# A six-layer mixer on one core: linear-attention stages over three tiles and one instead of two and two, and a new order of all steps

## What is computed

```
x = x + _L0_xattn_ref(_layernorm(x), ctx_1024, ...)        # local cross attention, 512 keys per batch
x = x + _L0_attn_ref(_layernorm(x), ...)                   # a decaying scan over time
x = x + _L0_ffn_ref(_layernorm(x), ...)                    # shared network and 2 of 8 experts
x = x + _L1_xattn_ref(_layernorm(x), ctx_1024, ctx_1024, mask, ...)   # full attention, 16 heads, masked
x = x + _L1_attn_ref(_layernorm(x), ...)                   # linear attention and a 512-wide network
x = x + _L1_ffn_ref(_layernorm(x), ...)                    # 1 of 16 experts, 32 slots each
```

```
ln1 = layer_norm(x, gamma1, beta1)
q, k, v = ln1 @ wq, ln1 @ wk, ln1 @ wv                     # 16 heads of 8
qp, kp = relu(q) + 0.001, relu(k) + 0.001
kvs = einsum('blhm,blhd->bhmd', kp, v)                     # per batch and head
num = einsum('blhm,bhmd->blhd', qp, kvs)
den = einsum('blhm,bhm->blh', qp, sum(kp, axis=1))
add1 = (num / den) @ wo + x
h = gelu(layer_norm(add1) @ w1 + b1)
out = gelu(h @ w2 + b2) + add1
...
pos = cumsum(onehot, axis=0) - 1                           # a token's place in its expert: counts all tokens before it
keep = pos < cap
```

## Time and profile before

| | us |
|---|---|
| median of 3 runs | 247.67 (247.62 to 248.0) |
| the profiled execution | 247.71 |
| its span | 245.6 |
| PE busy | 224.0 (91%) |
| DVE busy | 179.5 (73%) |
| ACT busy | 133.0 (54%) |
| POOL busy | 28.9 (12%) |

### The profile page before, as it was taken

The page is one execution under the profiler, slowest core; times in us unless marked ns, Lnnn a source line. Parts: engine busy times, 40 slices in busy tenths (PEclk is TensorE's granted clock), DMA queues, the critical chain, the costliest instruction groups (busy, mean ns, idle before and its releaser), DMA issues.

```text
span 245.6 us, 5281 instructions
## 1 busy us (share of the span) xinstructions
PE 224.0 (91%) x1996; PEld 157.9 (64%) x1996; DVE 179.5 (73%) x518; ACT 133.0 (54%) x289; POOL 28.9 (12%) x47
## 2 busy tenths in 40 slices
PE   7899999998998997669799999989999888898995
PEld 6322785585965866436568666657667677787485
DVE  2574716999857389999786978998988757834672
ACT  2205651274566073579999796979858361133030
POOL 3010001010223033021302210010000111201000
PEclk9999999999999599999999999999999999999999
DMA  7999949200000000060004200000008998000001
GB/s 220 419 435 423 429 152 227 60 0 0 4 0 0 0 3 1 0 167 7 0 3 109 65 4 3 0 4 0 3 0 344 434 451 358 3 0 0 3 3 43
DMA packets 2904, 26.87 MB, mean 109 GB/s; under 512 B 448, under 2 KB 704, under 8 KB 1344
## 3 DMA queue, kind: packets, MB, share of 16 engines
q1 hardware_dynamic: 2880, 26.54, 29.8%
HBM read 26.28 MB, written 0.26 MB: 108 GB/s over the span
## 4 chain that ended last, share of the span: by engine, by line
PE 61%; DVE 21%; issue 9%; ACT 4%; POOL 1%; DMA 1%; POOLq 0%; DVEq 0%; ACTq 0%
PE bank L1403 9%; PE bank L1389 6%; PE bank L1279 5%; PE bank L1257 5%; PE bank L1218 4%; DVE ctx_sb L946 4%; PE bank L1419 4%; PE bank L1362 2%; PE bank L1202 2%; PE bank L1345 2%; PE bank L1614 2%; PE bank L1288 2%; PE bank L1604 1%; PE bank L1588 1%; ACT ctx_sb L557 1%
## 5 line engine op out<-in xcount | busy, mean ns | idle before, releaser
L557 ACT ACTIVATE ctx_sb<-ctx_sb,small_sb 128x512 f32<-128x512 f32 x64 | 46.0, 722 | 13.3 <-DVE small_sb L946 13.1
L946 DVE CUSTOM_DVE_ANT_0 ctx_sb<-bank,mask_sb 128x512 f32<-128x512 f32 x64 | 41.8, 683 | 4.0 <-PE bank L1389 3.9
L1403 PE MATMUL bank<-early_sb,ctx_sb 128*128 128x128 f32 x256 | 35.8, 278 | 3.1 <-ACT work_sb L568 1.8
L1403 PEld LDWEIGHTS bank<-early_sb,ctx_sb 128*128 128x128 f32 x256 | 27.8, 141 | 14.3 <-ACT ctx_sb L557 7.8
L377 POOL TENSOR_TENSOR rstd_sb<-veps_sb,minus_half_sb 128x2 f32<-128x2 f32 (+1 forms) x13 | 10.3, 791 | 145.9 <-DVE veps_sb L643 117.0
L568 ACT COPY work_sb<-bank 128x512 f32<-128x512 f32 x40 | 22.5, 577 | 3.9 <-PE bank L1403 3.7
L1389 PE MATMUL bank<-k_sb,work_sb 32*128 32x512 f32 x128 | 18.6, 639 | 3.9 <-DVE small_sb L946 3.9
L706 DVE SCALAR_TENSOR_TENSOR work_sb<-bank,early_sb,work_sb 128x512 f32<-128x512 f32 x16 | 11.9, 747 | 9.4 <-PE bank L1257 8.9
L1222 PEld LDWEIGHTS bank<-late_sb,ctx_sb 128*128 128x128 f32 x128 | 15.2, 191 | 5.1 <-issue 5.0
L957 DVE COPY work_sb<-bank 128x512 f32<-128x512 f32 x24 | 16.5, 687 | 2.7 <-PE bank L1403 2.7
L1222 PE MATMUL bank<-late_sb,ctx_sb 128*128 128x128 f32 x128 | 16.4, 280 | 1.6 <-DVE v_sb L749 1.4
(11 more groups left out here) (260 smaller groups left out, 396.5 us busy)
## 6 DMA issues: line engine op xcount, KB each, us to landing
k_sb<-moe_w SPq DMA_DIRECT2D x1, 4096.0 KB, 12.5
ctx_sb<-moe_w SPq DMA_DIRECT2D x1, 4096.0 KB, 15.7
ctx_sb<-ctx SPq DMA_DIRECT2D x3, 1024.0 KB, 15.2
late_sb<-late SPq DMA_DIRECT2D x1, 2966.5 KB, 21.7
mask_sb<-ctx_tok SPq DMA_DIRECT2D x1, 2048.0 KB, 13.2
v_sb<-ctx_tok SPq DMA_DIRECT2D x1, 2048.0 KB, 27.6
mask_sb<-mask SPq DMA_DIRECT2D x4, 512.0 KB, 8.3
mask_sb<-mask SPq DMA_DIRECT2D x8, 256.0 KB, 4.5
```

The costliest lines, as they stand in the source:

```text
L557: s.activation(sc[u % NSC], sc[u % NSC], ACT.Exp, bias=smin[:, u:u + 1], scale=-1.0, accum_out=rsum[:, u:u + 1]).then_inc(sig("p1_ready"), 1)
L946: v.tensor_tensor_reduce(sc[u % NSC], bank[SB[u % GROUPS]][:, :], mask[:, KEYS * b:KEYS * (b + 1)], MASK_BIG, 3e38, ALU.add, ALU.min, smin ...
L1403: last = nc.tensor.transpose(bank[TB[u % 2]][:, P * k:P * (k + 1)], sc[u % NSC][:, P * k:P * (k + 1)], wt("ident"))
```

## The change

Stream c takes tiles 0 to 2 (twelve batches), d tile 3 (four batches). Both have buffers of their own, and c can start only when 48 of the 64 exponentials are done. In c, the values are copied to SBUF by ACT and masked for four batches at once on POOL, three times; key-value products, their masks and denominators run for three tiles; the four hidden products go one by one through one bank, each with bias and GELU in one ACT operation from PSUM, where before two banks were filled by two products each and a GELU over all four followed. In both stages: the second of the two norms is formed directly by one power of var * (1 + eps) + eps * eps' (the first no longer has to be multiplied in), so that POOL does two powers of one column a tile and the three DVE steps between fall away; the bias b2 goes in by a product with the identity and the GELU reads PSUM; key sums are read in PSUM; the token dispatch mask is formed with the test for capacity in one operation. In d the gate's bias goes in by a product as well. Heads are taken for batches 12 to 14 and for 15 apart, the last from another bank. `dispatch(0, j)` moves to the end of c. Copies of transposed units go to DVE for 2 in 8 units, not 3. All four orders are new, from the first steps on.

The diff, cut (the orders of DVE, ACT and POOL, and slices that only follow the new tile counts, are left out):

```diff
 TURNS = {
     "PE": (
-        "L2 P L10 P L P5 L P L8 P L2 a L2 P L3 a L2 a3 L P L P7 L P L a L6 a L a2 L P a b P2 a3 b a3 b P b P "
-        "a P a P2 S P4 T S b P S T2 b T b T2 S V T b T b T2 S b T2 b V T b S T b3 T2 V T2 V S T b T2 b T S T2 "
-        "V T2 V S T4 V T2 c T2 S V T2 S T2 V T2 c T2 S V T4 c S V T2 c T2 c S V T2 c S T2 c T2 c T2 c S V c V "
-        "T2 c T2 V T2 c V c d3 c G8 d c d4 G d G3 d G2 d c d c G6 c G d G2 d6 G4 d G2 d2 G5 d G4 d19 "),
+        "L2 P L10 P L P5 L P L8 P L2 a L2 P L3 a L2 a2 L a L P7 L P2 L a L5 a L a2 L P2 a L P a P a2 b a3 b "
+        "P2 b a b a P2 S P2 S P2 T b P S T4 b T b T2 S V T b T S V b T2 b V b S T b T2 b3 T4 S V T2 b T S T2 "
+        "b T V T V T2 S T2 V T2 S T2 V T2 S T4 S V T2 V T2 S T2 V T2 c T2 V T2 S V c T2 S T2 c T c V c T2 S T "
+        "c T2 V c T2 c V c d2 c d G c G c d4 G d G c G c d3 c G c d c d c2 d3 G2 c G c d G3 d G4 c d2 G7 c2 "
+        "d19 "),
...
+        LT, LB = (range(0, 3), range(3, 4)), (12, 4)
+        def lcols(h):
...
-        mg = [kvs, mask[:, MH:MH + 4 * HTOK]]
-        ksum = small[:, 832:832 + HB]
+        def linear_buffers(n, at, rd):
+            (qp, att, qk, kp_tok, add1, res4, g2, vb, kvs), end = part(mask, [P * n] * 7 + [4 * P * n] * 2, at)
+            return (qp, att, qk, kp_tok, add1, res4, g2, vb, kvs, small[:, rd:rd + HEADS * n]), end
+        lin0, at = linear_buffers(3, 0, 560)
+        assert at <= MH + MH // 2
+        lin1, at = linear_buffers(1, MH + MH // 2, 608)
+        assert at <= CTX
+        lin = (lin0, lin1)
...
-        BY_DVE = (1, 4, 7)
+        BY_DVE = (3, 7)
...
             def linear_stages(h):
-                inverse_std(h, tiles_of(h), extra=True)
-                yield
...
+                yield
+                inverse_std(h, LT[h])
+                yield
+                for t in LT[h] if not h else ():
+                    pool.wait_ge(sig("vt_ready"), 1)
+                    g.tensor_tensor(vb[:, 512 * t:512 * (t + 1)].rearrange("p (b d) -> p b d", b=4),
+                                    att[:, P * t:P * (t + 1)].unsqueeze(1).broadcast_to([P, 4, P]),
+                                    wt("batchof").unsqueeze(2).broadcast_to([P, 4, P]), ALU.mult).then_inc(sig("vb_ready"), 1)
+                    yield
+                inverse_std(h, LT[h])
+                yield
+                g.tensor_tensor(res4, x_tok[:, lcols(h)], add1, ALU.add).then_inc(sig("res_ready"), 1)
+                yield
+                inverse_std(h, LT[h])
                 yield
...
             def linear_stages(h):
-                A, B = XL[h], YL[h]
-                normT(h, lnT[:, cols(h)], A[:, HTOK:], scale=wt("gamma"), bias=wt("beta"))
...
+                normT(h, lnT[:, c], turnedT, scale=wt("gamma"), bias=wt("beta"))
                 yield
                 act.wait_ge(sig("vtok_ps"), h + 1)
-                if h:
-                    s.copy(vb[:, 0:HTOK], B[:, 0:HTOK]).then_inc(sig("vtok_ready"), 1)
...
-                normT(h, lnT[:, cols(h)], A[:, HTOK:], scale=wt("gamma"), bias=wt("beta"))
+                s.copy(vb[:, 0:P] if h else att, B[:, 0:NT]).then_inc(sig("vtok_ready" if h else "vt_ready"), 1)
+                yield
+                normT(h, lnT[:, c], turnedT, scale=wt("gamma"), bias=wt("beta"))
                 yield
                 for n in range(4):
-                    act.wait_ge(sig("ffh_ps"), 2 * h + n // 2 + 1)
-                    s.activation(hT[:, HTOK * n:HTOK * (n + 1)], (B, A)[n // 2][:, HTOK * (n % 2):HTOK * (n % 2 + 1)],
-                                 ACT.Gelu if h else ACT.Identity, bias=wt("b1")[:, n:n + 1]).then_inc(sig("ffh_ready"), 1)
-                    yield
-                if not h:
-                    act.wait_ge(sig("ffh_ready"), 4)
-                    s.activation(hT, hT, ACT.Gelu).then_inc(sig("gelu_ready"), 1)
-                    yield
-                act.wait_ge(sig("ffo_ready"), h + 1)
-                s.activation(g2, g2, ACT.Gelu).then_inc(sig("g2_ready"), 1)
-                yield
-                normT(h, lnT[:, cols(h)], A[:, HTOK:])
+                    act.wait_ge(sig("ffh_ps"), 5 + n // 2 if h else n + 1)
...
                 ts = slice(tiles.start, tiles.stop)
+                if extra is not None:
+                    second = slice(TT + tiles.start, TT + tiles.stop)
+                    norms[h] += 1
+                    v.tensor_scalar(veps[:, second], ag3[:, ts, 1], 1.0 + extra, eps * extra, ALU.mult, ALU.add)\
+                        .then_inc(sig(f"ln_var{h}"), 1)
+                    yield
...
-                    v.tensor_scalar(veps[:, second], veps[:, second], extra, None, ALU.add).then_inc(sig(f"ln_var{h}"), 1)
+                v.tensor_scalar(veps[:, ts], ag3[:, ts, 1], eps, None, ALU.add).then_inc(sig(f"ln_var{h}"), 1)
...
+            def normalize_once(ch, h, src3, tiles, dst3):
+                dve.wait_ge(sig(f"ln_rstd{h}"), norms[h])
                 for t in tiles:
                     ch.add(v.tensor_scalar(dst3[:, t, :], src3[:, t, :], ag3[:, t, 0:1], rstd[:, t:t + 1],
                                            ALU.subtract, ALU.mult))
...
+                for n, (lo, hi) in enumerate(TAKE):
+                    dve.wait_ge(sig("o1_ready"), hi)
+                    src = bank[OB1][:, 0:P * (hi - lo)] if n < 4 else bank[OB2][:, 0:P]
+                    o = src.rearrange("p (b j q) -> p b j q", b=hi - lo, j=4)
+                    to = oT[:, SEQ * lo:SEQ * hi].rearrange("p (b q) -> p b q", b=hi - lo)
...
-                dve.wait_ge(sig("qk_ps"), h + 1)
...
-                ch.join()
-                dve.wait_ge(sig("vtok_ps"), h + 1)
+                dve.wait_ge(sig("oT_ready"), 5 if h else 3)
+                v.tensor_tensor(oT[:, c], oT[:, c], A[:, 0:NT], ALU.mult).then_inc(sig("o1T_ready"), 1)
+                yield
+                dve.wait_ge(sig(f"xo{k}_ps"), 4)
                 if not h:
-                    v.tensor_tensor(vb[:, 0:512].rearrange("p (b d) -> p b d", b=4),
-                                    vtok(0).unsqueeze(1).broadcast_to([P, 4, P]),
-                                    wt("batchof").unsqueeze(2).broadcast_to([P, 4, P]), ALU.mult).then_inc(sig("vb_ready"), 1)
-                    yield
+                    dve.wait_ge(sig("xb0_ready"), 2)
+                dve.wait_ge(sig("xb1_ready"), 2)
+                residual((ZL[1] if h else B)[:, 0:NT], xb_tok[:, c], k, c)
...
                 dve.wait_ge(sig("ksum_ps"), h + 1)
-                ch.add(v.tensor_copy(ksum, B[:, 0:HB]))
-                yield
-                ch.join()
-                v.tensor_tensor(bs(qk), bs(qp), ksum.unsqueeze(2).broadcast_to([P, HB, SEQ]), ALU.mult).then_inc(sig("qksum_ready"), 1)
+                ksum = B[:, 0:nb] if h else B[:, NT:NT + nb]
+                v.tensor_tensor(qk.rearrange("p (b s) -> p b s", s=SEQ), qp.rearrange("p (b s) -> p b s", s=SEQ),
+                                ksum.unsqueeze(2).broadcast_to([P, nb, SEQ]), ALU.mult).then_inc(sig("qksum_ready"), 1)
...
+                yield
+                wait_norm(k)
+                if h:
+                    for i in range(2):
+                        for m in (2 * i, 2 * i + 1):
+                            last = mm((B, A)[i][:, NT * (m % 2):NT * (m % 2 + 1)], wt("w1")[:, P * m:P * (m + 1)], lnT[:, c],
+                                      start=True, stop=True)
+                        last.then_inc(sig("ffh_ps"), 1)
+                        yield
+                else:
+                    for m in range(4):
+                        if m:
+                            pe.wait_ge(sig("ffh_ready"), m)
+                        mm(A[:, 0:NT], wt("w1")[:, P * m:P * (m + 1)], lnT[:, c], start=True, stop=True).then_inc(sig("ffh_ps"), 1)
+                        yield
+                pe.wait_ge(sig("ffh_ready"), 6 if h else 4)
+                ffo = B if h else A
+                for t in range(n):
+                    mm(tile_ps(ffo, t), wt("ident"), wt("b2"), start=(t == 0), stop=False, skip_group_check=True)
+                for m in range(4):
+                    if h and m > 1:
+                        pe.wait_ge(sig("ffh_ready"), 5 + m)
+                    for t in range(n):
+                        last = mm(tile_ps(ffo, t), hT[:, NT * m + P * t:NT * m + P * (t + 1)], wt("w2")[:, P * m:P * (m + 1)],
+                                  start=False, stop=(m == 3), skip_group_check=True)
+                    if m == 1:
                         yield
                 last.then_inc(sig("ffo_ps"), 1)
                 yield
+                turn_lnT(k, many, tiles)
...
+                dst, hot = count_ps(h), mr[5]
+                if h:
+                    pe.wait_ge(sig("onehot_ready"), 1)
+                    for t in range(3):
+                        mm(dst, wt("ones"), hot[:, E1 * t:E1 * (t + 1)], start=(t == 0), stop=False, skip_group_check=True)
+                    yield
+                    pe.wait_ge(sig("onehot_ready"), 2)
```

(10 more changed lines are left out.)

335 lines of the change are left out of this document (141 added, 194 removed), and 16 rows, old and new, of the table TURNS.

## The result

The changed kernel took 255.67 us in the median of four executions: 252.77, 253.71, 257.63 and 261.69, against 247.64 for the kernel before on the same chip. The ratio of 1.023 (1.016 to 1.029) compares the two shortest, the undisturbed ones, with the kernel before. In the same order the four had mean granted clocks of 0.973, 0.973, 0.953 and 0.934. The forecast was 245.0, range 242.3 to 248.8: the wrong side, and outside the range.

A forecast was written before the change was run, and what follows sets the result against it. It took PE as the bound before (at half speed) and in the attention, and a chain of some fifty dependent steps in the last linear stage. 247.71 - 2.5 - 1.5 + 2.0 - 0.7 = 245.0 us, range 242.3 to 248.8.

The forecast's parts named there:

- part 1: Before the attention: a projection and more full-height work ahead of the clock's fall avoid most of it, -2.5 us.
- part 2: Attention up to the 48th transposed unit: stream c's first steps leave, ACT becomes the fullest engine, -1.5 us.
- part 3: From the 48th transposed unit to the end of the attention: steps 1 to 8 of c move in, +2.0 us.
- part 4: After the last output product: shorter d, longer c, walked in order to 35.4 us against 36.1, -0.7 us.
- the 0.94 us gap: PE's wait for DVE's copy of the routing weights, ahead of 8-row products and the clock's fall; a projection would fill it.
- the stretch of 104 to 107 us: Row taken as support for the new order: PE busy 1.21 of 3.0 us at clock 1.00, with full-height products.
- the clock falls all the same: Rival: the new order does not prevent the fall before the attention; 247.5 us, 246 to 249, chance 0.25.
- DVE becomes the path: Rival, end of the attention: DVE's copies of transposed units stand behind c's wide steps; 249.0 us, chance 0.16.
- a fall elsewhere (the tail has fewer fillers): Listed sign that the prediction is wrong: the clock falls at another place; no size given.
- c, not d, sets the end: Last linear stage: three-tile c runs beside d and takes back 7.7 us of d's 8.4 us gain.
- the masks on GpSimd are free: Key-value masks moved to GpSimd, costed at nothing; up to 3 x 0.6 us if their cover is gone.
- the table load has no drain behind it: GELU table load on c's path costed at 1.28 us by the trace; with the skill's drain the sum would be 246.3.

The follow-up runs named there:

- e5: Changed kernel with full contraction rows, 27 filler turns after the last output product and 13 fillers around 93 to 103 us; 249.00 us, ratio 1.004.
- e1: Kernel before, with half a's 8-row and 64-row products contracting over all 128 rows, added rows zero; 245.13 us, ratio 0.989.
- e2: Kernel before, without the 76 filler records of its last linear stage; 254.34 us, ratio 1.025.
- e4: Changed kernel with 27 more filler turns after the last output product and full contraction rows; 249.17 us, ratio 1.007.
- e12: Changed kernel with full contraction rows and no filler added; 257.23 and 257.80 us, ratio 1.040.
- e9: e5 with the three tiles' hidden products alternating between two banks, PE, ACT and DVE orders adapted, 9 fillers fewer; 245.43 us, ratio 0.991.
- e8: e5 with each of the three key-value masks on GpSimd computed twice; 248.58 us, ratio 1.004 against the kernel before.
- e6: Kernel before with full contraction rows as in e1, plus 16 fillers between 93 and 106 us and 12 in the last stage; 245.14 us, ratio 0.988.

## Why the prediction was wrong

In the two shortest executions, 253.2 us in the mean, the forecast was 8.2 us short. The parts below, with parts 1 to 3 as in the profiled execution and part 4 as in e5 with the clock held, make 6.4 of it: 2.7 for a gain that never came (part 1), -0.2 (part 2), 0.4 (part 3), 3.5 for the walk of the last stage (part 4). So some 2 us, an estimate, are left for falls behind the first scores. In the profiled execution that last term is 10.3.

**Part 1 (-2.5 us, measured +0.15).** The price was right, the remedy not. Without the fall the stretch to the first scores is 3.2 us shorter in the old order (e1) and 2.8 in the new one (from the same transpose, 17.30 us in the changed kernel and 14.50 in e5). But the fall didn't hang on the 0.94 us gap. The step that failed is the sentence that takes the stretch of 104 to 107 us as evidence for the new order. That row (PE busy 1.21 of 3.00 us at clock 1.00) says that the clock had not fallen by then. It doesn't say that such work holds it. e2, the same program up to there, has a fall at just that place (103.0), and e1 and e4 have theirs at 100.6 and at 96.0. This was the rival "the clock falls all the same", and it had 0.25.

**Part 2 (-1.5, measured -1.7; -1.6 at full clock)** held, and ACT was indeed the fullest engine: 19.61 of the last 19.91 us of this stretch, against PE's 19.31 (window from 148.00 above).

**Part 3 (+2.0, measured +2.4).** Right size, wrong engine. PE was busy 25.39 of 26.72 us, where the sum had 22.9: c's products at three tiles take some 8.2 us of PE in this stretch, not 6.3 (in e5, from each start to the next: 1.27 for the row products, 0.78 + 0.66 for the projection, 0.67 for the transposes, 0.86 + 0.78 + 0.65 for key, value and query, 0.58 for the key sums, 0.96 + 1.03 for two key-value products: 8.24). DVE's 22.07 is what was forecast (22.6), and the copies it owns cost PE 0.5 us at one place in e5. That the size came out is partly luck: most of the time that the walk had put down to the engines blocking each other was PE's own work. The rival "DVE becomes the path" did not happen.

**Part 4 (-0.7, measured +13.2 in the profiled execution, +2.8 with the clock held).** Two steps failed.
The first was never costed: the clock in the tail. The last paragraph of the prediction names it ("a fall elsewhere (the tail has fewer fillers)"), but no rival carried it and no range reached it. It is 10.3 us in the profiled execution (49.23 against 38.90 and 38.88), some 2 in the two shortest by the sum above, and 8.7 in e12, whose two executions agree. It comes once more in e2 by taking the fillers out of the kernel before. The count was in the change: 30 fewer filler records, and spread thin.
The second is the walk of c's chain. Up to the GELU's table it is right: in e5, after the last output product, the transposed input is there at 12.6 (predicted 12.5), the table at 13.9 (13.8). The last GELU ends at 20.4 instead of 18.8: 1.0 because the second product waits behind d's steps in PE's order, and 0.6 because the product is 0.91 us, not 0.65. The masks end at 35.4 instead of 32.6, so a further 1.2 us lies in the output products, norms and routing, and the dispatch products take 3.4 instead of 2.8. Together 38.9 for 35.4. With two banks and their order (e9) the stage is 35.81.

Some of the prediction's sums don't come out, without bearing on the 245.0. The bound of part 3, 7.8 us less the 1.52 that PE stood, is 6.3 and not 5.3, which would put the DVE rival at 250. In part 4, thirty steps at 0.08 to 0.15 us are 2.4 to 4.5 us and not 5. The walk's four numbers for the hidden products fit only as the starts of the second, third and fourth product and of the last GELU. And a measurement of this kernel doesn't tell 0.5 us: its executions ranged over 4.2 to 6.5 us on each of three chips.

That c, not d, sets the end, that the masks on GpSimd are free (e8), and that the table load has no drain behind it all held. For the last: the load started at 204.03 in e5, 0.02 us behind the operation ahead of it, and took 1.28 us, and the GELU started at 205.33. "ScalarE: Activation LUTs" in the Trainium skill, What ACT_TABLE_LOAD costs, adds about 1.38 us of drain; the trace doesn't agree here, on the path this time. Against e5, which has the clock that the forecast assumed, the forecast of 242.9 us of span is 3.3 short (246.2), nearly all of it in this part's walk.

What stays open: why one program has a fall in one execution and not in another, as at 103 us, and where the two shortest executions of the changed kernel had theirs; what each of the 8-row and the 64-row products does to the clock, since e1 changed both; and whether the 32-row products in the last stage have a part in its falls, since only fillers were tried there.

## What to carry to other kernels

Where the granted clock falls once in a trace, cost a fall as a term of its own in every stretch in which a change thins out PE's work: here it was worth some 3 us before the attention and, in the tail, from some 2 us (an estimate) to 10 us, where the whole rearrangement was forecast to gain 2.7. Count the fillers in a diff as you count the work, and pad short contractions with zero rows where the weights have them anyway. When one stream is made wider to make another shorter, look for the place where the wide one goes through a single buffer: that chain grows with each tile, and a second bank with the order that goes with it won back 2.8 of the 3.6 us of span by which the change was behind at full clock (e5, e9 against e6).
